# Decoder layer, one core: squared lengths from the norm's statistics, bias added by GpSimd, first values moved one batch forward

## What is computed

```
x = x + attention(layernorm(x))       # 16 heads of 16; weight (q.k)**2, causal, divided by its sum
x = x + aligned(ctx, layernorm(x))    # D = sqrt(|c|^2 + |n|^2 - 2 c.n), dynamic time warping over D,
                                      # backtracked path; each context row is added to the tokens on its path
x = x + ffn(layernorm(x))             # 256 -> 1024, butterfly, gelu, butterfly, -> 256, with two output biases
layernorm(x) = (x - m) / sqrt(v + 1e-5)
```

## Time and profile before

| | |
|---|---|
| median of 3 runs | 864.7 us (864.68 to 865.21) |
| the profiled execution | 866.8 us, span 865.1 us |
| PE busy | 780.7 us, 90% of the span |
| PE's granted clock, mean | 0.97 of 2.4 GHz |
| ACT / DVE / POOL busy | 445.7 / 479.3 / 137.1 us |
| PE in the chain that ended last | 71% |

### The profile page before, as it was taken

How to read it: one execution, slowest core, us unless ns; L and a number is a source line. 1 busy time by engine, 2 the same in 40 slices (tenths; PEclk the granted TensorE clock), 3 DMA queues, 4 the chain that set the end, 5 groups by cost and what they waited for, 6 DMA issues and landing times.

```text
span 865.1 us, 12185 instructions
## 1 busy us (share of the span) xinstructions
PE 780.7 (90%) x3991; PEld 384.6 (44%) x3991; DVE 479.3 (55%) x1915; ACT 445.7 (52%) x679; POOL 137.1 (16%) x330
## 2 busy tenths in 40 slices
PE   4886799889999888899999999878899999999998
PEld 3352233224433334333334332444367467558567
DVE  5646455542455322399999897436799885140000
ACT  1245786776687664797876877431510311350220
POOL 2220322311222111122331223000000000200200
PEclk9998999899999998999999999879899999999999
DMA  4383324302234311123340332000110113000001
GB/s 153 127 238 125 93 103 159 110 1 74 75 88 144 112 39 55 24 90 125 114 159 9 89 93 53 14 8 1 38 44 25 35 36 71 12 1 25 24 13 36
DMA packets 53146, 61.29 MB, mean 71 GB/s; under 512 B 21391, under 2 KB 32323, under 8 KB 53083
## 3 DMA queue, kind: packets, MB, share of 16 engines
q1 hardware_dynamic: 49819, 54.22, 20.9%
q0 software_dynamic: 1088, 4.19, 1.5%
q10 hardware_dynamic: 2176, 2.10, 0.7%
HBM read 37.17 MB, written 23.32 MB: 70 GB/s over the span
## 4 chain that ended last, share of the span: by engine, by line
PE 71%; DVE 9%; ACT 9%; issue 4%; DMA 4%; SPq 2%; ACTq 0%; POOL 0%; DVEq 0%
PE psW L1468 13%; PE psS L1452 13%; PE psO L1305 13%; PE psS L1288 12%; PE psW L1357 5%; ACT ARENA L868 4%; PE psW L1380 4%; PE psW L1364 2%; PE psW L1389 2%; SPq L623 2%; PE psW L1392 2%; DMA qk_parts<-ARENA 2%; PE psW L1442 1%; PE psW L1348 1%; DVE FOLD L1017 1%
## 5 line engine op out<-in xcount | busy, mean ns | idle before, releaser
L868 ACT ACTIVATE ARENA<-psS 128x1024 f32<-128x1024 f32 (+3 forms) x384 | 299.7, 812 | 106.0 <-PE psS L1288 103.5
L1288 PE MATMUL psS<-ARENA 96*128 96x512 bf16 (+3 forms) x768 | 187.4, 335 | 26.0 <-ACT ARENA L868 24.8
L788 POOL TENSOR_SCALAR_AFFINE_SELECT ARENA<-ARENA 128x256 f32<-128x256 f32 x256 | 109.1, 430 | 406.4 <-ACT ARENA L868 404.4
L1305 PE MATMUL psO<-ARENA 128*32 128x512 f32 (+3 forms) x1536 | 167.9, 509 | 3.9 <-ACT ARENA L873 3.7
L1288 PEld LDWEIGHTS psS<-ARENA 96*128 96x128 bf16 x768 | 56.0, 99 | 209.2 <-ACT ARENA L868 123.0
L1468 PE MATMUL psW<-W2E,ARENA 128*128 128x256 f32 x512 | 115.4, 382 | 0.4 <-ACT ARENA L889 0.4
L1468 PEld LDWEIGHTS psW<-W2E,ARENA 128*128 128x128 f32 x512 | 95.6, 189 | 19.3 <-issue 5.8
L945 ACT ACTIVATE ARENA<-psS,BEFF 128x512 f32<-128x512 f32 x64 | 43.4, 687 | 90.2 <-PE psS L1452 90.2
L1357 PE MATMUL psW<-XX,ARENA 128*128 128x512 f32 x128 | 66.3, 620 | 5.3 <-DVE ARENA L1168 3.6
L1452 PE MATMUL psS<-XX,MIXA 128*128 128x512 f32 x128 | 58.9, 615 | 3.7 <-ACT ARENA L945 2.7
L1305 PEld LDWEIGHTS psO<-ARENA 128*32 128x32 f32 x1536 | 30.6, 109 | 67.7 <-issue 41.2
(11 more groups left out here) (147 smaller groups left out, 849.2 us busy)
## 6 DMA issues: line engine op xcount, KB each, us to landing
ARENA<-qk_parts SPq DMA_DIRECT2D x192, 128.0 KB, 2.7
qk_parts<-ARENA SPq DMA_DIRECT2D x16, 768.0 KB, 3.4
X<-in_x POOLq DMA_DIRECT2D x3, 1024.0 KB, 7.3
dist<-ARENA SPq DMA_DIRECT2D x1, 2560.0 KB, 8.1
MORE<-dist SPq DMA_DIRECT2D x16, 160.0 KB, 2.2
out<-ARENA ACTq DMA_DIRECT2D x8, 256.0 KB, 2.1
out<-ARENA SPq DMA_DIRECT2D x8, 256.0 KB, 2.1
path<-MORE SPq DMA_DIRECT2D x16, 80.0 KB, 2.0
```

The lines of the kernel that those rows point to most:

```text
L788: pool.affine_select(out=blk, in_=blk, compare_op=ALU.is_ge, fill=0.0, base=0, pattern=[[0, 2], [1, P]], channel_multiplier=-1).then_inc(s ...
L868: nc.scalar.activation(A[:, (2 * G + a) % A_PAIRS, :, 0:N], psS[:, a, :, 0:N], ACT.Square).then_inc(s_sq, 1)
L1288: ins = nc.tensor.matmul(psS[:, a, j, 0:N], KST[0:STACK, g % 2, 2 * a + j, kt * P:(kt + 1) * P], QST[0:STACK, g % 2, 2 * a + j, q0:q0 + N] ...
L1305: ins = nc.tensor.matmul(psO[32 * j:32 * j + 32, o % 2, q0 - qc * HALF:q0 - qc * HALF + N], V1[:, kt, GH * g + j], A[:, (2 * G + j // 2) % ...
```

## The change

Four things are changed together.

1. **Squared lengths.** `rstd` of the student norm also makes LESS = -256 * 1e-5 * rstd^2 (one small DVE operation per half or whole batch), `order` adds 256 to AA (one small DVE operation per batch), and `dist` sums four matmuls of 128 columns, LESS broadcast over 103 columns as the weights and the identity as the moving side, in place of the two of 512 columns with ones. `turn_s` makes the copy alone. PE waits for LESS on a new semaphore.
2. **Bias.** POOL adds the bias to x of batches 0 and 1 in place, once their FFN norm has been read; the single-row matmuls of `out` are gone, and `out` waits for POOL.
3. **Order.** The first two `value` units of each next batch stand in the last attention steps of the batch in front; `context` and `order` units are set apart among the `up` units and the norm of batch 1; around the end of batch 3 `along` of batch 1, one `hidden` unit and `dist(3, 1)` stand earlier; pauses are adjusted.
4. **Start.** x of batch 0 comes in two DMAs, and its norm and its turns run in two halves; `bits` (a DVE table) comes after them.

```diff
@@ make_plan
-    plan = norm_units("x", 0, 0) + [("bits",)] + turns(0) + [("coef", i) for i in range(3)] + side[:4]
+    (s0, n0), (s1, n1) = half_parts("x", "turn_x", 0, 0)
+    plan = s0 + s1[:2] + n0[:3] + s1[2:] + n0[3:] + n1[:3] + [("coef", 0), ("coef", 1)] + n1[3:] + [("bits",), ("coef", 2)] + side[:4]
...
+    with_values = lambda last, b: last[:-2] + [last[-2] + values(b)[:1], last[-1] + values(b)[1:2]]
...
-    plan += flat(spread(steps[:-3], fill)) + flat(steps[-3:-1]) + both(1) + steps[-1]
+    plan += flat(spread(steps[:-3], fill)) + flat(with_values(steps[-3:-1], 1)) + both(1) + steps[-1]
...
-    plan += along_other[:2] + wo(3)[2:3] + other[:2] + ahead[:1] + wo(3)[3:] + early_hidden[:SOON - 1] + ahead[1:7] + other[4:6]
-    plan += ahead[7:-1] + early_hidden[SOON - 1:] + ahead[-1:] + other[6:] + [("turn_f", 1, i) for i in range(4)]
+    plan += along_other[:2] + early_hidden[:1] + wo(3)[2:3] + other[:2] + ahead[:1] + wo(3)[3:] + early_hidden[1:] + ahead[1:7] + other[4:6]
+    plan += ahead[7:] + other[6:] + second_base + [("turn_f", 1, i) for i in range(4)]
@@ sync
-            sp.dma_start(X[:, 0], x[0].rearrange("(t p) d -> p t d", p=P)).then_inc(s_x_in[0], 16)
+            for h in range(2):
+                sp.dma_start(X[:, 0, 4 * h:4 * h + 4], x[0].rearrange("(t p) d -> p t d", p=P)[:, 4 * h:4 * h + 4]).then_inc(s_x_rest if h else s_x_in[0], 16)
@@ gpsimd, "base"
+                    pool.wait_ge(s_xn, max(normal_of["ffn", b, i] for i in range(TT // 2)) + 1)
+                    pool.wait_ge(s_bias, 1)
...
+                    pool.tensor_tensor(out=X[:, b] if b < PAIR else XB, in0=X[:, b], in1=BIAS[:].unsqueeze(1).to_broadcast([P, TT, D]), op=ALU.add
@@ scalar, "turn_s"
-                    nc.scalar.activation(SNT[:, k, h * HALF:(h + 1) * HALF], psW[:, bank(*u)], ACT.Copy)
-                    nc.scalar.activation(SQT[:, k, h * HALF:(h + 1) * HALF], psW[:, bank(*u)], ACT.Square).then_inc(s_free[bank(*u)], 1)
+                    nc.scalar.activation(SNT[:, k, h * HALF:(h + 1) * HALF], psW[:, bank(*u)], ACT.Copy).then_inc(s_free[bank(*u)], 1)
@@ vector, "rstd"
+                    if what == "student":
+                        inverse = RS[later(what, b)][:, t0:t1]
+                        nc.vector.scalar_tensor_tensor(out=LESS[:, b, t0:t1], in0=inverse, scalar=-D * LN_EPS, in1=inverse,
+                                                       op0=ALU.mult, op1=ALU.mult).then_inc(s_less, 2 * (t1 - t0) // TT)
@@ tensor, "dist"
-                        for k in range(KD):
-                            ins = nc.tensor.matmul(W[0:SPAN], ONES[:, 0:SPAN], SQT[:, k, cols], start=False, stop=k == KD - 1)
+                        pe.wait_ge(s_less, 2 * b + h + 1)
+                        for t in range(4):
+                            ins = nc.tensor.matmul(W[0:SPAN, t * P:(t + 1) * P], LESS[:, b, 4 * h + t:4 * h + t + 1].to_broadcast([P, SPAN]), IDENT[:],
+                                                   start=False, stop=t == 3)
@@ tensor, "out"
-                        pe.wait_ge(s_bias, 1)
+                        pe.wait_ge(s_base, b + 1)
...
-                            nc.tensor.matmul(sums, ONES[0:1], BIAS[0:1], start=False, stop=False)
```

More of the change, by code:

```diff
@@ L140 @@
 HALVED = ("qk", "value", "wo", "dist")
-SIZE = dict(qk=17, value=17, wo=17, dist=34, turn_x=5, turn_s=5, turn_f=5, along=9, up=5, w1=5, down=9, chain=5, coef=9, context=2, order=2, w_exp=5,
-            mix=9, bias=4, stats=3, variance=2, root=1, rstd=1, normal=3, pause=4)
+SIZE = dict(qk=17, value=17, wo=17, dist=30, turn_x=5, turn_s=5, turn_f=5, along=9, up=5, w1=5, down=9, chain=5, coef=9, context=2, order=2, w_exp=5,
+            mix=9, bias=4, stats=3, variance=2, root=1, rstd=1, normal=3, pause=4, base=0)
 VECTOR = dict(qk=18, wo=7, along=7, stats=8, variance=12, rstd=2, normal=8, forward=8, backward=8, moves=12, meet=65, half=0)
@@ L221, in make_plan @@
     qk = lambda b: [("qk", b, i) for i in range(8)]
+    with_values = lambda last, b: last[:-2] + [last[-2] + values(b)[:1], last[-1] + values(b)[1:2]]
     two = lambda a, b: flat([x, y] for x, y in zip(a, b))
     nx, links = norm_x(1), chain(1)
-    fill = (up + context + nx[:4] + order + nx[4:5] + pairs(0, 8)[:2] + nx[5:6] + pairs(0, 8)[2:] + nx[6:] + turns(1)
-            + two(qk(1), pairs(0, 9)) + [("bias",)] + qk(1)[4:5] + w1 + two(links, qk(1)[5:]) + links[3:]
+    fill = (flat([up[2 * i], up[2 * i + 1], context[i]] for i in range(B)) + nx[:2] + order[:1] + nx[2:4] + order[1:2] + nx[4:5] + pairs(0, 8)[:1]
+            + order[2:3] + nx[5:6] + pairs(0, 8)[1:2] + order[3:] + nx[6:] + pairs(0, 8)[2:] + turns(1)
+            + two(pairs(0, 9), qk(1)) + [("bias",)] + qk(1)[4:5] + w1 + two(links, qk(1)[5:]) + links[3:]
             + pairs(1, 9) + pairs(1, 8) + pairs(1, 7) + [("down", i) for i in range(HT // 2)])
     steps = steps_of(0)
-    plan += flat(spread(steps[:-3], fill)) + flat(steps[-3:-1]) + both(1) + steps[-1]
+    plan += flat(spread(steps[:-3], fill)) + flat(with_values(steps[-3:-1], 1)) + both(1) + steps[-1]
     nx, ns0, v, w = norm_x(2), norm_units("student", 0), values(1), wo(0)
-    fill = (v[:2] + w[:2] + nx[:4] + v[2:3] + nx[4:5] + v[3:] + nx[5:6] + w[2:3] + nx[6:] + w[3:] + ns0[:4] + turns(2)
-            + qk(2)[:2] + ns0[4:5] + qk(2)[2:4] + ns0[5:6] + qk(2)[4:6] + ns0[6:] + qk(2)[6:] + [("pause",)] * 3
+    fill = (w[:2] + nx[:4] + v[2:3] + nx[4:5] + v[3:] + nx[5:6] + w[2:3] + nx[6:] + w[3:] + ns0[:4] + turns(2)
+            + qk(2)[:2] + ns0[4:5] + qk(2)[2:4] + ns0[5:6] + qk(2)[4:6] + ns0[6:] + qk(2)[6:] + [("pause",)] * 6
             + [("turn_s", 0, 0), ("turn_s", 0, 1), ("dist", 0, 0)])
@@ L236, in make_plan @@
     plan += flat(spread(steps[:-8], fill, {**value_due(1), **wo_due(0)}))
-    plan += flat(spread(steps[-8:-1], hb[:5] + [("turn_s", 0, 2), ("turn_s", 0, 3)] + hb[5:6] + [("dist", 0, 1)] + hb[6:]))
+    plan += flat(with_values(spread(steps[-8:-1], hb[:5] + [("turn_s", 0, 2), ("turn_s", 0, 3)] + hb[5:6] + [("dist", 0, 1)] + hb[6:]), 2))
     plan += both(2) + steps[-1]
@@ L392, in layer @@
         RS = [sb("RS", [P, TT]), sb("RS2", [P, TT])]
+        LESS = sb("LESS", [P, B, TT])
         CORNER = sb("CORNER", [LANES, 1])
@@ L501, in layer @@
         s_x_in = [sem(f"s_x_in{b}") for b in range(B)]
+        s_x_rest = sem("s_x_rest")
         s_ready = sem("s_ready")
@@ L633, in dist_out @@
                     sp.dma_start(by_row(dist_dram, b, way)[:, blocks],
-                                 BACK[b][3][rows_of(way)].rearrange("p (w c) -> p w c", c=CB)[:, blocks]).then_inc(s_dist_out[b][h][way], 16)
+                                 BACK[b][2][rows_of(way)].rearrange("p (w c) -> p w c", c=CB)[:, blocks]).then_inc(s_dist_out[b][h][way], 16)
             def path_out(w, g):
@@ L1126, in _ @@
                         dve.wait_ge(s_x_in[b], 16)
+                    if what == "x" and (b, i) == (0, 2):
+                        dve.wait_ge(s_x_rest, 16)
                     if what == "student":
```

42 lines of the change are left out of this document (20 added, 22 removed).

## The result

The changed kernel takes 843.0 us (median of four runs, 842.6 to 844.1) against 865.0 for the kernel before, beside it on the same chip: ratio 0.973 [0.970, 0.976], some 22 to 23 us less. The forecast was 835.5 us, so the sign and the range hold and about a quarter of the expected gain is missing. The profiled execution has a span of 840.9 us, against 865.1.

What follows compares the result with a forecast made beforehand. PE, busy 90% of the span, was taken as the bound, with DVE's second-warp chain ending within 1.7 us of PE's FFN work. Terms summed to -29.2 us from 864.7, giving 835.5 us, range 820 to 853.

Steps and rivals of the forecast that it cites:

- The bound: Second warp to first `along` of batch 2: PE's FFN work and DVE's chain end within 1.7 us of each other.
- `dist`, ACT: Smaller `dist` matmuls save 0.8 us in each of 8 units, -6.4 us; removing ACT's squares gives -3.5 us.
- Batch 0 and the start: Reordered units in batch 0 give -5 us despite a new 2 to 5 us context wait; start in halves gives -2.5.
- What follows on PE, and SP's stacks behind it, move with it: Start: PE's first turns move from 12.05 to about 9.5 us, and the work behind them comes earlier too; -2.5 us.
- Values ahead: Starts of batches 1 to 3: earlier `value` units fill PE's waits, 2.08 us at batch 2; -3 us.
- needs nothing from attention: Start of batch 2: `value`, 1.7 us of PE work independent of attention, can fill PE's 2.08 us wait.
- End of batch 3: Around the end of batch 3: units fill waits of 3.87 and 2.71 us, distances go out 1.7 us sooner; -6.7 us.
- two `along` units and a product: End of batch 3: some 2.7 us of PE work as filling for the 3.87 us wait.
- (a): Rival: holes in attention don't close because ACT or a DMA is late next; 848 us, chance 0.24.
- (b): Rival: PE stays the bound to the end because the second warp starts still earlier; 825 us, chance 0.10.
- (d): Rival: new `dist` matmuls, one-column weights read 103 times, run slower; 874 us at 0.5 us more per record, chance 0.04.
- (c): Rival: POOL's second `base` holds up DVE's first rows of the second warp up to 4.5 us; 840 us, chance 0.04.

Runs made afterwards that it cites:

- my own last edit: Third of three order changes to the changed kernel: FFN-norm statistics of batch 1 moved later around batch 3's end; measured only with the other two, 835.8 us.
- the context ahead: Changed kernel with the context's DMA issued at the start, ahead of the stacks on SP's queue: 838.8 us, 0.967 of the kernel before.
- the root ahead: Changed kernel with the root of batch 1's second-half student norm one unit earlier, ahead of value(2, 2): 839.1 us, 0.970 of the kernel before.
- three moves: Changed kernel with context DMA and student-norm root earlier, and batch 1's FFN-norm statistics later around batch 3's end: 835.8 us, 0.965 of the kernel before.
- the longer warp: Changed kernel with 16 settings of an unused tile on DVE between forward and backward rows of the second warp: 849.6 us, 0.982 of the kernel before.

## Why the prediction was right, and what it missed

- *The bound.* Right, and the most useful step: DVE's chain and PE's work ended within 1.7 us, so removing PE work beside the chain would turn into a wait. The wait was forecast at 8.1 us and measured at 9.65, because a half `out` unit gave 0.82 us (9.43 to 7.79 us for a unit) and not 0.7. The restart behind it costs about 1.8 us (from that `along` to the first one of batch 3 takes 33.9 us, before 33.7, though two halves without bias save 1.6 of it), forecast 2. The row-to-end span is 253.4, forecast 254. For the bias in all -1.1 was forecast; in place the profiles give 1.5.
- *`dist`, ACT.* Right in kind and in the 0.9 us of a unit, and -12 alone (-16 to -8) agrees with -9.9. In the part's own trace the waits of `dist` for ACT fell from 3.4 to 1.6 us and those of the scores from 24.8 to 23.0, about the 3.5 forecast. In the changed kernel the first are 3.4 again, 1.68 us of it at batch 1's end and 0.90 at `dist(3, 1)`.
- *Batch 0 and the start.* -5 was right (-6 alone), as was the wait at the context of "2 to 5 us" (1.96 and 4.03). The start's -2.5 wasn't: alone it measured nothing. **The step that failed is "What follows on PE, and SP's stacks behind it, move with it".** The queue did move, the context's DMA by 1.7 to 2.0 us against the kernel before. But alone, PE's 2.3 us at the first turns were 1.3 at the first attention step, 1.4 at the turns of batch 1, and gone behind them in a stretch at the lower clock. In the changed kernel the wait that the part on batch 0 opened takes up whatever PE gains ahead of it, as the two profiles of it show. Both terms lead to that one DMA, and the sum counted them as if each stood alone.
- *Values ahead.* -3 was -1.7 alone. The step failed at "needs nothing from attention": true for PE, but taking two units out of the list brought `turn_s(1, 2)` forward, and ACT's root stood behind the remaining one. The wait that took its place, 2.8 to 3.1 us, is larger than the one removed.
- *End of batch 3.* -6.7 was -1.6 alone (-3.0 to -0.1), the largest miss of the sum. The step that failed is the 3.87 us taken as filled by "two `along` units and a product", with the 1.7 us for overtaking a unit. The hole was 2.38 us still, `along` waited 1.65 for ACT's copy, and the overtaken unit was the cover of ACT's copies, so that `dist(3, 1)` waited 1.88.
- *Rivals.* What came is between the forecast and (a), holes that reopen on ACT or a DMA (848). (b) didn't come: the wait shows it. (d) didn't: 0.11 us a record. Its threshold was miscounted, though: it left out the 6.4 us that `dist` itself saves. Slower begins at 29.2 / 64 = 0.46 us more per record, not 0.36, and 0.5 more gives 867.5 us, not 874. (c) as told didn't: the second addition on POOL runs 580.64 to 585.15 us, 2.4 ahead of the first row. The outer bounds of 818 and 858 us aren't sums of the bounds given, which lead to about 825 and 855; the range stated doesn't rest on them.

## What to carry to other kernels

Find the point where two engines' long chains meet, and read every version by two numbers, when the later chain starts and how long it is from there to the end: thirteen profiles here agree on the second within 3 us (252.9 to 255.7), and only the one with the longer chain doesn't; the first explains the rest. When a unit is moved in an ordered list, look at what each of its engines has queued behind it: both the hole that the values opened at the start of batch 2 and the failure of my own last edit were a root of 0.2 us that stood behind, or in front of, somebody else's copies. Before a gain at the start is counted, follow it to the next wait for a transfer, and compare single profiles with care: the first attention step of kernels with the same start stood 2.4 us apart.

## What was not expected of the hardware

The first addition on POOL did disturb DVE, in another place than (c) said. DVE's scalar addition on 16 columns in the last `heads_out` takes 0.175 us in the median of 32; in the changed kernel the last takes 1.76 us and ends when POOL's does. Its DVE and POOL:

```profile
564.13 1.76 DVE L977 TENSOR_SCALAR ZT<-ARENA 128x16 f32<-128x16 f32 x1
```

```profile
561.34 4.52 POOL L818 TENSOR_TENSOR X<-X,BIAS 128x2048 f32<-128x2048 f32 x1 [6.87 <-DVE XX L1164]
```

and DVE in the kernel with the bias back on PE, where POOL has no such work:

```profile
563.83 0.17 DVE L979 TENSOR_SCALAR ZT<-ARENA 128x16 f32<-128x16 f32 x1
```

The statistics and the transposition that DVE ran beside the same POOL operation kept their usual times. In four later kernels (the context ahead, the root ahead, three moves, the longer warp) the same operation takes 2.25 us, and PE waits 1.55 at the output projection behind it; with the bias on PE there is no such wait. The Trainium skill ("SBUF — State Buffer", Who interferes with whom) names DVE's `tensor_scalar` among the operations that can take the pair of ports shared with GpSimd, when its operands meet the conditions of a 2-port mode, and says that the later one blocks for the whole instruction of the other; the trace agrees, 1.76 against 0.17 us, though it doesn't show the ports or the mode themselves. The prediction had used the part on two inputs alone, and had called the addition free. Moving it behind the second warp's first row wasn't tried, and isn't known to be free there either, since the rows have two inputs.
